# Attention and gated FFN on one core: another order for the LayerNorm prologue and for the first group's KV units

## The chip, the cores and the metric

One core of a Trainium2 chip. The metric is the device time of one execution in microseconds, lower is better; the median of three runs of the kernel before is 1325.37 us (1324.14 to 1325.52).

## The reference, cut to what matters

```python
xn = _layernorm(x)                        # x: 1024 tokens x 512
q = xn @ Wq.T                             # 32 heads of 128
k = xn @ Wk.T; v = xn @ Wv.T              # 8 groups of 128, four heads share one
q = rmsnorm(q, q_norm_w); k = rmsnorm(k, k_norm_w)
scores = q k^T / sqrt(128) + slope * (k_pos - q_pos), causal
s = softmax(scores) v @ Wo.T
g = silu((silu(xn @ gate) * (xn @ up)) @ down)     # gate, up, down dequantised from integers
return x + s * g
```

## The kernel before, in words

Every fp32 operand of a product is split in two parts, hi (rounded to the matmul's fp32r) and lo (the rest). ScalarE writes the hi part, VectorE or GpSimd (POOL) the lo part, and TensorE (PE) runs three products, hi*hi, hi*lo and lo*hi.

**Prologue.** SyncE loads the eight tiles of x (128 tokens each, L285), while ScalarE's own queue loads the KV weights of group 0 (L536). For each tile VectorE computes the statistics (`ln_stats`, L635, and `ln_variance`, L640 to L643), two tiles at a time; POOL takes the power -0.5 (L414) and normalises both rows in place (`ln_rows`, L417). PE transposes the normalised tile (`ln_transposes`, L1012), ScalarE writes `xh` (L547) and VectorE `xl` (`ln_lo`, L650). PE has 14 + 1 + 3 matmuls on zeros (`idle_matmuls`, L1005) before and between the first two transposes and the first product. A "KV unit" (`kv_proj`, L967) is 24 matmuls of 256 columns that give K and V of two token tiles; a "Q unit" (`q_proj`, L950) is 12 matmuls of 512 columns that give Q^T of one head for 512 tokens, called qc1 for the later half of the tokens and qc0 for the earlier. The order of PE's units in the prologue stands in `PRO`: kv0, kv1, kv2, the Q unit qc1_0, kv3, with the transposes of later x tiles placed inside the units. K of group 0 is copied from PSUM by VectorE (L751), squared and summed by ScalarE (`k_squares`, L518), and scaled by POOL (`k_norm`, L403 and L406); then PE transposes it (`first_k_transposes`) and ScalarE and VectorE split it (L530, L735).

**Heads.** A group has four heads. Within a head eight query tiles (idx 0 is the last tile, 1024 keys long) pass through scores (PE, L926 to L929), logits (VectorE adds the bias tile that POOL made, L687), exp (ScalarE, L497), normalise (VectorE, L693 and L696), transposes of the probabilities (PE, `lot`, L907), their split (ScalarE L487, VectorE L671) and the product with V (PE, `values`, L945). Between these PE's queue holds projections: the Q units of this and the next head, the output projection of the two heads before (`w_unit`; in heads 0 and 1 there is none yet), and one KV unit of the next group per head (kv0 to kv3 of group 1 in heads 0 to 3). The order is written out by hand on each engine; `group_order` gives the sequence in which the two PSUM banks `O` are handed on, and `Places` turns it into semaphore counts. A unit waits until the one before it in this list has left its bank's partner (`take`, L892). The first group is written apart from the six steady ones (a loop over heads, unrolled) and the last, which has no KV units. The feed-forward part follows and is not touched.

Of the kernel before, what the change touches and what calls it, by code (L numbers as in the profile page):

```python
# [111 lines left out]
PRO = ["kv0", "kv1", "kv2", "qc1_0", "kv3"]  # L112


def group_order(first, last):


    out = []
    for j in range(PER):
        nx = (j + 1) % PER  # L120
        more = not (last and j == PER - 1)
        prev, w = not (first and j == 0), not (first and j < 2)
        out += [f"qc0_{j}"] + [f"v0_{j}"] * prev + [f"w0_{j}", f"w1_{j}"] * w
        if first and j == 0:
            out += ["kv0", "qc1_1"]
# [56 lines left out]
def f(ap):  # L182

    return ap.bitcast(F32)
# [10 lines left out]
def attention(nc, stack, keep, x, wq, wkv, wo, slopes, qkw, mats, down_sc):  # L195
# [32 lines left out]
    rstd = sb("rstd", [P, QT])  # L228
    kss, kms, kinv = sb("kss", [P, QT]), sb("kms", [P, QT]), sb("kinv", [P, QT])
# [8 lines left out]

    LN_BANKS = [T[0][:, :], T[1][:, :]] + [S[n // 2][:, n % 2 * CH:(n % 2 + 1) * CH] for n in range(4)]
# [5 lines left out]
    setup, ln_st, ln_mv, ln_var, ln_rstd, xn_ready = (  # L245
        sem("setup"), sem("ln_st"), sem("ln_mv"), sem("ln_var"), sem("ln_rstd"), sem("xn_ready"))
# [81 lines left out]
    def _(pool):  # L328
# [70 lines left out]
        def k_norm(g, c):  # L399
            n = NC * g + c  # L400
            cs = slice(c * CT, (c + 1) * CT)
            pool.wait_ge(kms_ready, n + 1)
            g_.tensor_tensor(kinv[:, cs], kms[:, cs], cst[:, 0:1].to_broadcast([P, CT]),  # L403
                             ALU.pow).then_inc(kinv_ready, 1)
            pool.wait_ge(kinv_ready, n + 1)
# [4 lines left out]
        def ln_rows(n):  # L410
# [69 lines left out]
    def _(act):  # L480
# [55 lines left out]
        act.dma_start(wkv_in[:, :, :], wkv[0]).then_inc(wkv_ld, 16)  # L536
        act.wait_ge(wkv_ld, 16)
        for n in range(2):
            ks = slice(2 * n, 2 * n + 2)
            a_.activation(wkv_h[:, ks, :], wkv_in[:, ks, :], ACT.Copy).then_inc(wkv_hi, 1)  # L540
        wq_hi_part(0)
# [8 lines left out]
        ln_hi(range(0, 5))  # L550
        k_squares(pro, ["kv0"], 0)
        ln_hi(range(5, 7))
        k_squares(pro, ["kv1"], 0)
        ln_hi(range(7, 8))
        k_squares(pro, ["kv2"], 0)
        q_hi(pro, "qc1_0")
# [3 lines left out]
        k_squares(pro, ["kv3"], 0)  # L560
        wkv_hi_part(1)

        def group(g, kind):
# [4 lines left out]
            for j in range(PER):  # L568
# [10 lines left out]
                q_hi(at, f"qc0_{j}")  # L579
                if kind == "first" and j == 0:  # L580
                    act.wait_ge(kt_ready, 2)
                    kT_hi_part(0, slice(CH, TOK))
                if j == 0:
                    exp(h, 0)
# [22 lines left out]
                if kind != "last":  # L607
# [3 lines left out]
                lots(h, 2)  # L611
                v_hi(at, f"v1_{j}", j)
# [16 lines left out]
    def _(dve):  # L629
# [35 lines left out]
        ln_lo(range(3, 4))
# [105 lines left out]
        def group(g, kind):
# [6 lines left out]
            for j in range(PER):  # L778
# [17 lines left out]
                elif kind == "first":  # L796
                    q_lo(at, f"qc0_{j}")
                    dve.wait_ge(kt_hi, 2)
                    kT_lo_part(slice(CH, TOK))
                    logits(h, 0)  # L800
# [41 lines left out]
                if not last and (prev or j > 0):  # L842
# [6 lines left out]
                lots(h, 3)  # L849
                normalise(h, 6)  # L850
# [26 lines left out]
    def _(pe):  # L877
# [53 lines left out]

        def values(at, name, h, wait, between=None):
# [67 lines left out]
        pro = Places("pro")  # L1000

# [5 lines left out]
        def ln_transposes(i):  # L1007
            pe.wait_ge(xn_ready, i + 1)
# [6 lines left out]

        pe.wait_ge(warm, 1)
# [522 lines left out]
```

## Time and profile before

| | us |
|---|---|
| median of 3 runs | 1325.37 |
| profiled execution, its own time | 1325.52 |
| its span, first to last instruction | 1323.4 |
| PE busy | 1287.3 (97%) |
| VectorE (DVE) busy | 970.1 (73%) |
| ScalarE (ACT) busy | 649.8 (49%) |
| GpSimd (POOL) busy | 710.2 (54%) |

All times in the trace are from the span's start. PE rows are matmuls, PEld rows weight loads. The last entry in brackets is how long the engine sat idle before the instruction, and who released it. Matmul durations overlap (they are pipelined), so lengths of stretches of PE are read from start to start.

### The profile page before, as it was taken

The numbers are of one execution on the slowest core, as the hardware profiler recorded it, in microseconds if no ns is written. First come the engines' busy times: TensorE is split into PE (matmuls) and PEld (weight loads), VectorE is DVE, ScalarE is ACT, GpSimd is POOL, SyncE is SP. The second block draws the span as 40 slices with busy tenths as digits, with TensorE's granted clock in tenths as the row PEclk, the third lists the DMA queues.
The fourth block names the chain that finished last, engine by engine and source line by source line (L and its number), as shares of the span: only waits on it lengthen the run. The fifth ranks groups of instructions, "written<-read, shape, count | busy, mean of one in ns | idle before, by whom it ended". The sixth has DMA issues, their size and how long they took to land. (4 is left out here: it accounts for less than half of the span.)

```text
span 1323.4 us, 20983 instructions
## 1 busy us (share of the span) xinstructions
PE 1287.3 (97%) x7138; PEld 1105.0 (83%) x7138; DVE 970.1 (73%) x2072; ACT 649.8 (49%) x1422; POOL 710.2 (54%) x755
## 2 busy tenths in 40 slices
PE   7899999999999999999999999999999989999997
PEld 6778888888888888888888888888888878888886
DVE  4678787778777877787778777877788855555556
ACT  3555565556555555555555555555565523222222
POOL 8645464546455545554555455545555625555553
PEclk8899999999999999999999999999999999999999
DMA  3000000000000000100000000000020036455441
GB/s 121 17 17 17 33 17 17 17 32 17 17 17 32 17 17 17 33 17 17 17 33 17 17 16 33 17 17 17 17 64 20 5 77 194 128 127 127 127 127 64
DMA packets 29468, 57.88 MB, mean 44 GB/s; under 512 B 3648, under 2 KB 3648, under 8 KB 29248
## 3 DMA queue, kind: packets, MB, share of 16 engines
q1 hardware_dynamic: 29232, 56.16, 14.9%
q8 instruction: 54, 0.88, 0.3%
q10 hardware_dynamic: 144, 0.52, 0.1%
q14 instruction: 38, 0.31, 0.1%
HBM read 54.57 MB, written 2.10 MB: 43 GB/s over the span
## 5 line engine op out<-in xcount | busy, mean ns | idle before, releaser
L396 POOL TENSOR_TENSOR pb<-rel,coef 128x1024 f32<-128x1024 f32 (+7 forms) x256 | 293.7, 1162 | 123.9 <-PE T L907 118.1
L497 ACT ACTIVATE pb<-pb,low 128x1024 f32<-128x1024 f32 (+7 forms) x256 | 198.9, 777 | 188.6 <-DVE low L687 186.9
L487 ACT ACTIVATE pt_h<-T 128x512 fp32r<-128x512 f32 (+3 forms) x384 | 185.9, 486 | 115.0 <-PE T L907 111.6
L671 DVE TENSOR_TENSOR pt_l<-T,pt_h 128x512 fp32r<-128x512 f32 (+3 forms) x384 | 210.4, 551 | 41.2 <-ACT pt_h L487 41.1
L687 DVE CUSTOM_DVE_ANT_0 pb<-S,pb,ninv 128x1024 f32<-128x1024 f32 (+7 forms) x256 | 207.8, 812 | 40.7 <-PE S L929 35.8
L907 PE MATMUL T<-ident,pb 128*128 128x128 f32 x1152 | 190.7, 275 | 14.9 <-DVE pb L696 8.4
L907 PEld LDWEIGHTS T<-ident,pb 128*128 128x128 f32 x1152 | 141.6, 141 | 53.6 <-issue 14.0
L696 DVE TENSOR_SCALAR pb<-pb,rinv 128x1024 f32<-128x1024 f32 (+7 forms) x256 | 172.5, 674 | 9.0
L926 PE MATMUL S<-kT_h,q_h 128*128 128x512 f32 (+2 forms) x384 | 142.0, 370 | 0.0
L945 PE MATMUL O<-pt_h,v_h 128*128 128x512 f32 (+2 forms) x384 | 140.7, 366 | 1.0 <-DVE pt_l L671 1.0
L373 POOL TENSOR_TENSOR inv<-ms,cst 128x4 f32<-128x4 f32 x64 | 76.2, 1191 | 120.8 <-DVE ms L719 120.8
L352 POOL TENSOR_TENSOR wo_l<-wo_in,wo_h 128x512 fp32r<-128x512 f32 x32 | 41.5, 1297 | 184.3 <-ACT wo_h L534 184.3
L945 PE MATMUL O<-pt_h,v_l 128*128 128x512 f32 (+2 forms) x384 | 133.4, 347 | 0.0
L945 PE MATMUL O<-pt_l,v_h 128*128 128x512 f32 (+2 forms) x384 | 132.9, 346 | 0.0
L927 PE MATMUL S<-kT_l,q_h 128*128 128x512 f32 (+2 forms) x384 | 129.2, 344 | 0.0
L929 PE MATMUL S<-kT_h,q_l 128*128 128x512 f32 (+2 forms) x384 | 111.4, 344 | 0.0
L886 PE MATMUL O<-xh,wq_h 128*128 128x512 f32 x256 | 109.2, 427 | 0.7 <-DVE xl L650 0.7
L886 PE MATMUL O<-oT_h,wo_h 128*128 128x512 f32 x256 | 107.1, 418 | 0.0
L886 PE MATMUL O<-xh,wq_l 128*128 128x512 f32 x256 | 101.0, 394 | 0.0
L886 PE MATMUL O<-oT_h,wo_l 128*128 128x512 f32 x256 | 100.7, 393 | 0.0
L886 PE MATMUL O<-oT_l,wo_h 128*128 128x512 f32 x256 | 100.6, 393 | 0.0
L886 PE MATMUL O<-xl,wq_h 128*128 128x512 f32 x256 | 100.5, 393 | 0.0
(148 smaller groups left out, 2898.7 us busy)
## 6 DMA issues: line engine op xcount, KB each, us to landing
wq_in<-in_wq SPq DMA_DIRECT2D x32, 256.0 KB, 2.8
wo_in<-in_wo SPq DMA_DIRECT2D x32, 256.0 KB, 2.6
stage<-in_wkv SPq DMA_DIRECT2D x7, 512.0 KB, 3.9
stage<-in_gate_w SPq DMA_DIRECT2D x14, 256.0 KB, 2.6
stage<-in_gate_z SPq DMA_DIRECT2D x14, 256.0 KB, 3.6
stage<-in_gate_s SPq DMA_DIRECT2D x14, 256.0 KB, 5.2
stage<-in_up_w SPq DMA_DIRECT2D x14, 256.0 KB, 5.3
stage<-in_up_z SPq DMA_DIRECT2D x14, 256.0 KB, 6.4
```

The costliest lines, as they stand in the source:

```text
L396: g_.tensor_tensor(pbuf(idx, t), rel[:, TOK - w:TOK], coef[:, t:t + 1].to_broadcast([P, w]), ALU.mult).then_inc(bias_ready, 1)
L487: a_.activation(pt_lot(pt_h, t, n), bank[:, 0:m * P].rearrange("p (k w) -> p k w", w=P), ACT.Copy).then_inc(tr_hi, 1)
L497: a_.activation(pbuf(idx, t), pbuf(idx, t), ACT.Exp, bias=low[:, idx:idx + 1], scale=-1.0, accum_out=rsum[:, idx:idx + 1]).then_inc(exps_r ...
L671: v_.tensor_tensor(pt_lot(pt_l, t, n), bank[:, 0:m * P].rearrange("p (k w) -> p k w", w=P), f(pt_lot(pt_h, t, n)), ALU.subtract).then_inc( ...
L687: v_.tensor_tensor_reduce(out=pbuf(idx, t), in0=S[idx % 2][:, BASE[t]:BASE[t] + (t + 1) * P], in1=pbuf(idx, t), scale=ninv[:, t:t + 1], sc ...
L696: v_.tensor_scalar(pbuf(idx, t), pbuf(idx, t), rinv[:, idx:idx + 1], None, ALU.mult).then_inc(probs_ready, 1)
L886: ins = mm(out, a, b, start=(n == 0), stop=(n == 3 * len(terms) - 1))
L907: ins = nc.tensor.transpose(bank[:, k * P:(k + 1) * P], pbuf(idx, t)[:, (k0 + k) * P:(k0 + k + 1) * P], ident[:, :])
L926: mm(out, q[:, qs], kT_h[:, k0:k0 + w], start=True, stop=False)
L927: mm(out, q[:, qs], kT_l[:, k0:k0 + w], start=False, stop=False)
L929: ins = mm(out, q[:, qs], kT_h[:, k0:k0 + w], start=False, stop=True)
L945: ins = mm(o, v[:, kt, :], pt[:, a:a + w], start=(kt + i == 0), stop=(kt == n - 1 and i == 2))
```

## The change

The loads: `wkv[0]` is issued by SyncE between x tiles 3 and 4 and no longer by ScalarE at the start. LayerNorm rows 0, 1, 2, 4 and 6 are normalised by VectorE with the same two-scalar instruction that POOL had; rows 3, 5 and 7 by ScalarE as scale * x + shift, where POOL computes the shift, 128x1, from mean and rstd. POOL keeps the power and loses the eight 128x512 rows; of the KV weights' lo part it makes one half, VectorE the other. In kv0 the products with the lo weights come last, and the first ones wait for halves of the hi weights. The zero matmuls are 11 + 4 in place of 14 + 1 + 3. In the prologue kv3 comes before the Q unit qc1_0. K of group 0 is scaled by VectorE, tile by tile (eight instructions of 128x128), and POOL only takes the power. The first bias tile (128x1024) of head 0 is made by VectorE. The first scores of head 0 stand after 12 of the 24 matmuls of group 1's kv0, where they stood after 20, and their last products alone wait for the lo part of Q. Head 0 runs KV units kv0 and kv1 of group 1, head 1 runs kv2 and kv3, heads 2 and 3 none.

```diff
-PRO = ["kv0", "kv1", "kv2", "qc1_0", "kv3"]
+PRO = ["kv0", "kv1", "kv2", "kv3", "qc1_0"]
+FIRST_KV = (["kv0", "kv1"], ["kv2", "kv3"], [], [])
...
     def _(sp):
         for i in range(QT):
+            if i == 4:
+                sp.dma_start(wkv_in[:, :, :], wkv[0]).then_inc(wkv_ld, 16)
             sp.dma_start(xs[:, i, :], x[i]).then_inc(x_in[i], 16)
...
# POOL
-            for i in (2 * n, 2 * n + 1):
-                g_.tensor_scalar(xs[:, i, :], xs[:, i, :], mv[:, i, 0:1], rstd[:, i:i + 1], ALU.subtract,
-                                 ALU.mult).then_inc(xn_ready, 1)
+            if n > 0:
+                i = 2 * n + 1
+                g_.tensor_scalar(shift[:, i:i + 1], mv[:, i, 0:1], rstd[:, i:i + 1], -1.0, ALU.mult,
+                                 ALU.mult).then_inc(ln_shift, 1)
         pool.wait_ge(setup, SETUP + 5)
-        wkv_lo_half(0)
         ln_rows(0)
-        wkv_lo_half(1)
         ln_rows(1)
+        wkv_lo_first()
         ln_rows(2)
+        wq_lo(0)
         ln_rows(3)
-        wq_lo(0)
-        k_norm(0, 0)
+        k_inv(0, 0)
+        k_inv(0, 1)
         pool.wait_ge(tab_in, 32)
         norms(0, 1)
-        k_norm(0, 1)
-        bias(0, 0)
+        pool.wait_ge(bias_ready, 1)
         bias(0, 1)
...
# ScalarE
-        act.dma_start(wkv_in[:, :, :], wkv[0]).then_inc(wkv_ld, 16)
...
+        def ln_rows(i):
+            act.wait_ge(ln_shift, XN_ACT.index(i) + 1)
+            a_.activation(xs[:, i, :], xs[:, i, :], ACT.Identity, bias=shift[:, i:i + 1],
+                          scale=rstd[:, i:i + 1]).then_inc(xn_by_act, 1)
+        ln_hi(range(0, 1))
...
+        ln_hi(range(1, 2))
+        ln_rows(3)
+        ln_hi(range(2, 4))
+        wq_hi_part(0)
+        ln_rows(5)
+        ln_hi(range(4, 6))
         k_squares(pro, ["kv0"], 0)
...
+        ln_rows(7)
+        ln_hi(range(6, 8))
+        k_squares(pro, ["kv1", "kv2", "kv3"], 0)
...
# VectorE
+        def ln_rows(i):
+            dve.wait_ge(ln_rstd, i // 2 + 1)
+            v_.tensor_scalar(xs[:, i, :], xs[:, i, :], mv[:, i, 0:1], rstd[:, i:i + 1], ALU.subtract,
+                             ALU.mult).then_inc(xn_by_dve, 1)
...
+        ln_stats(range(2, 3))
+        ln_rows(0)
+        ln_rows(1)
+        ln_stats(range(3, 4))
         ln_variance(1)
...
+        ln_lo(range(1, 2))
+        ln_rows(2)
+        ln_stats(range(4, 5))
+        ln_lo(range(2, 4))
+        ln_stats(range(5, 6))
         ln_variance(2)
+        first_kv_copy(0)
+        ln_rows(4)
+        ln_stats(range(6, 8))
         ln_variance(3)
+        ln_lo(range(4, 6))
+        ln_rows(6)
+        first_kv_copy(1)
+        ln_lo(range(6, 8))
...
+        def first_k_norm(c):
+            dve.wait_ge(kinv_ready, c + 1)
+            for k in range(c * CT, (c + 1) * CT):
+                ins = v_.tensor_scalar(kv[:, k, 0:HD], kv[:, k, 0:HD], kinv[:, k:k + 1], None, ALU.mult)
+            ins.then_inc(kn_ready, 1)
...
+                    dve.wait_ge(coef_ready, 2)
+                    v_.tensor_scalar(pbuf(0, TILES[0]), rel[:, :], coef[:, QT - 1:QT], None, ALU.mult
+                                     ).then_inc(bias_ready, 1)
...
# PE
         pe.wait_ge(warm, 1)
-        idle_matmuls(14)
+        idle_matmuls(11)
         pe.wait_ge(setup, SETUP + 5)
         ln_transposes(0)
-        idle_matmuls(1)
         ln_transposes(1)
-        idle_matmuls(3)
-        for n in range(3):
-            kv_proj(pro, f"kv{n}", 0, {6: [lambda n=n: ln_transposes(2 * n + 2)], 18: [lambda n=n: ln_transposes(2 * n + 3)]})
+        idle_matmuls(4)
+        first_kv0()
+        for n in (1, 2):
+            kv_proj(pro, f"kv{n}", 0, {8: [lambda n=n: ln_transposes(2 * n + 2)], 16: [lambda n=n: ln_transposes(2 * n + 3)]})
+        kv_proj(pro, "kv3", 0)
         pe.wait_ge(tr_lo, QT)
-        q_proj(pro, "qc1_0", 0)
-        kv_proj(pro, "kv3", 0, {4: [lambda: first_k_transposes(0)],
-                                14: [lambda: squares(pro.hi("qc1_0"), 1, QT, T[1])]})
+        q_proj(pro, "qc1_0", 0, {4: [lambda: first_k_transposes(0)]})
...
-                q_proj(at, "qc0_0", 0)
-                kv_proj(at, "kv0", 1, {6: [lambda: first_k_transposes(1)], 20: [first_scores]})
+                q_proj(at, "qc0_0", 0, {8: [lambda: squares(pro.hi("qc1_0"), 1, QT, T[1])]})
+                kv_proj(at, "kv0", 1, {2: [lambda: first_k_transposes(1)], 12: [first_scores]})
...
-                if not last and (prev or j > 0):
-                    kv_proj(at, f"kv{j}", g + 1, {3 * KT: [squares1]})
+                now = FIRST_KV[j][j == 0:2 - j] if kind == "first" else [f"kv{j}"] * (not last)
+                if now:
+                    kv_proj(at, now[0], g + 1, {3 * KT: [squares1]})
                 elif more:
                     squares1()
                 scores(h, 6)
                 lots(h, 3)
+                if kind == "first" and j == 1:
+                    kv_proj(at, "kv3", 1)
                 values(at, f"v1_{j}", h, g + 1 if j == 0 else None, {12: [lambda h=h: lots(h, 2)]})
```

## Rows read from the trace of the kernel before

**Rows 1.** The page: the span, and part 1, busy time of each engine.
```profile
span 1323.4 us, 20983 instructions
PE 1287.3 (97%) x7138; PEld 1105.0 (83%) x7138; DVE 970.1 (73%) x2072; ACT 649.8 (49%) x1422; POOL 710.2 (54%) x755
```

**Rows 2.** Waits of PE, 0 to 200 us: us in total, times, longest.
```profile
PE T L1012 <- POOL s_acc L417: 4.5, 3, 3.3
PE T L907 <- DVE pb L696: 3.2, 4, 1.8
PE T L907 <- DVE pt_l L671: 3.1, 4, 1.1
PE T L964 <- DVE pt_l L671: 1.8, 1, 1.8
PE O L886 <- DVE w_l L769: 1.2, 1, 1.2
PE S L1012 <- POOL s_acc L417: 1.1, 2, 0.7
PE O L886 <- DVE xl L650: 0.7, 1, 0.7
```

**Rows 3.** Timeline of PE: start us, us, line, operation, count, [idle before <-releaser].
```profile
1.58 6.25 PE L1005 MATMUL O<-pt_h 128*128 128x512 f32 x14 [1.58 <-DVE pt_h L653]
11.12 1.08 PE L1012 MATMUL T<-ident,s_acc 128*128 128x128 f32 x4 [3.30 <-POOL s_acc L417]
...
22.12 0.66 PE L1012 MATMUL S<-ident,s_acc 128*128 128x128 f32 x4 [0.70 <-POOL s_acc L417]
...
50.53 1.32 PE L907 MATMUL T<-ident,pb 128*128 128x128 f32 x8 [1.82 <-DVE pb L696]
...
65.44 0.63 PE L964 MATMUL T<-ident,sq 128*128 128x128 f32 x4 [1.81 <-DVE pt_l L671]
```

**Rows 4.** DMA issues, 0 to 60 us: KB each, median us from issue to landing.
```profile
s_acc<-in_x SPq DMA_DIRECT2D x8, 256.0 KB, 5.7
...
stage<-in_wkv ACTq DMA_DIRECT2D x1, 512.0 KB, 5.2
```

**Rows 5.** Windows: busy us of PE, PEld, DVE, ACT, POOL; granted clock; DMA share; GB/s.
```profile
7.00:8.00 1.00, 0.83 (x3) 0.20 (x1) 0.97 (x5) 0.06 (x1) 0.97 (x1) 1.00 1.05 404
...
11.00:12.00 1.00, 0.88 (x5) 0.91 (x5) 0.00 (x0) 0.63 (x1) 1.00 (x1) 0.50 0.19 58
...
17.50:18.00 0.50, 0.50 (x5) 0.50 (x4) 0.00 (x0) 0.00 (x0) 0.50 (x1) 0.67 0.00 0
...
52.00:53.00 1.00, 1.00 (x5) 0.91 (x4) 0.66 (x2) 1.00 (x3) 0.00 (x0) 0.50 0.02 8
...
58.50:59.00 0.50, 0.50 (x4) 0.46 (x3) 0.50 (x2) 0.13 (x1) 0.50 (x1) 0.71 0.00 0
```

**Rows 6.** Timeline of all engines: statistics, power and rows of the first two tiles.
```profile
5.74 1.45 DVE L635 BATCH_NORM_STATS2 stats<-s_acc 128x6 f32<-128x512 f32 x2 [4.21 <-DMA s_acc<-in_x]
...
8.08 0.72 POOL L414 TENSOR_TENSOR rstd<-var_e,cst 128x2 f32<-128x2 f32 x1
8.90 4.14 POOL L417 TENSOR_SCALAR s_acc<-s_acc,mv,rstd 128x512 f32<-128x512 f32 x2
```

**Rows 7.** Timeline of PE: first matmuls of qc1_0, of kv3 and of qc0_0.
```profile
31.18 0.50 PE L886 MATMUL O<-xh,wq_h 128*128 128x512 f32 x1 [0.70 <-DVE xl L650]
...
34.03 0.28 PE L886 MATMUL O<-w_h,xh 128*128 128x256 f32 x1
...
37.76 0.40 PE L886 MATMUL O<-xh,wq_h 128*128 128x512 f32 x1
```

**Rows 8.** Timeline of DVE: one-input instructions, POOL idle and POOL busy.
```profile
65.39 0.49 DVE L696 TENSOR_SCALAR pb<-pb,rinv 128x512 f32<-128x512 f32 x1
...
71.24 1.37 DVE L696 TENSOR_SCALAR pb<-pb,rinv 128x256 f32<-128x256 f32 x1
```

**Rows 9.** Waits of PE, 940 to 1010 us, in the last group: us, times, longest.
```profile
PE T L907 <- DVE pt_l L671: 0.8, 2, 0.4
```

More of the change, by code:

```diff
@@ L123, in group_order @@
         out += [f"qc0_{j}"] + [f"v0_{j}"] * prev + [f"w0_{j}", f"w1_{j}"] * w
-        if first and j == 0:
-            out += ["kv0", "qc1_1"]
+        if first:
+            out += ["kv0"] * (j == 0) + [f"qc1_{nx}"] + [f"w2_{j}"] * w + FIRST_KV[j][j == 0:]
         else:
@@ L228, in attention @@
     rstd = sb("rstd", [P, QT])
+    shift = sb("shift", [P, QT])
     kss, kms, kinv = sb("kss", [P, QT]), sb("kms", [P, QT]), sb("kinv", [P, QT])
@@ L548, in ln_hi @@
                               ACT.Copy).then_inc(tr_hi, 1)
-        ln_hi(range(0, 5))
-        k_squares(pro, ["kv0"], 0)
[L552 to L556, printed above, removed]
+        def ln_rows(i):
[3 more added lines that the diff above has]
+        ln_hi(range(0, 1))
+        act.wait_ge(wkv_ld, 16)
+        for n in range(2):
+            ks = slice(2 * n, 2 * n + 2)
+            a_.activation(wkv_h[:, ks, :], wkv_in[:, ks, :], ACT.Copy).then_inc(wkv_hi, 1)
+        ln_hi(range(1, 2))
[4 more added lines that the diff above has]
+        ln_hi(range(4, 6))
+        k_squares(pro, ["kv0"], 0)
+        ln_rows(7)
+        ln_hi(range(6, 8))
+        k_squares(pro, ["kv1", "kv2", "kv3"], 0)
         act.wait_ge(qk_ready, 1)
@@ L559, in _ @@
         kT_hi_part(0, slice(0, CH))
-        k_squares(pro, ["kv3"], 0)
         wkv_hi_part(1)
+        q_hi(pro, "qc1_0")
         def group(g, kind):
@@ L582, in group @@
                     kT_hi_part(0, slice(CH, TOK))
+                q_hi(at, f"qc0_{j}")
                 if j == 0:
@@ L606, in group @@
                 exp(h, 5)
-                if kind != "last":
+                if kind == "first":
+                    k_squares(at, FIRST_KV[j][:2 - j], 1)
+                elif kind != "last":
                     k_squares(at, [f"kv{j}"], g + 1)
@@ L611, in group @@
                 lots(h, 2)
+                if kind == "first" and j == 1:
+                    k_squares(at, ["kv3"], 1)
                 v_hi(at, f"v1_{j}", j)
@@ L769, in _ @@
         v_.tensor_tensor(wkv_l[:, :, :], wkv_in[:, :, :], f(wkv_h[:, :, :]), ALU.subtract).then_inc(wkv_split, 1)
+        first_k_norm(1)
+        q_lo(pro, "qc1_0")
+        mean_sq(0, 1, QT, T[1])
         def group(g, kind):
@@ L841, in group @@
                 normalise(h, 5)
-                if not last and (prev or j > 0):
+                if kind == "first":
+                    kv_copy(at, FIRST_KV[j][j == 0:2 - j], 1)
+                elif not last:
                     kv_copy(at, [f"kv{j}"], g + 1)
@@ L849, in group @@
                 lots(h, 3)
+                if kind == "first" and j == 1:
+                    kv_copy(at, ["kv3"], 1)
                 normalise(h, 6)
@@ L930, in scores, with first_scores @@
             ins.then_inc(scores_ready, 1)
+        pro = Places("pro")
+        def first_scores():
+            qs = slice(TOK - P, TOK)
+            for k0 in range(0, TOK, CH):
+                pe.wait_ge(kt_lo, k0 // CH + 1)
+                ks = slice(k0, k0 + CH)
+                mm(S[0][:, ks], q_h[:, qs], kT_h[:, ks], start=True, stop=False)
+                mm(S[0][:, ks], q_h[:, qs], kT_l[:, ks], start=False, stop=False)
+            pe.wait_ge(out_free, pro.n("qc1_0"))
+            for k0 in range(0, TOK, CH):
+                ks = slice(k0, k0 + CH)
+                ins = mm(S[0][:, ks], q_l[:, qs], kT_h[:, ks], start=False, stop=True)
+            ins.then_inc(scores_ready, 1)
         def values(at, name, h, wait, between=None):
@@ L1106, in group @@
                 lots(h, 3)
+                if kind == "first" and j == 1:
+                    kv_proj(at, "kv3", 1)
                 values(at, f"v1_{j}", h, g + 1 if j == 0 else None, {12: [lambda h=h: lots(h, 2)]})
```

89 lines of the change are left out of this document (46 added, 43 removed).

## The prediction

> **What bounds the kernel now.** I read the page first: PE is busy 97% of a span of 1323.4 us, and VectorE, the next unit of work beside it, at 73% [rows 1]. So a change gains only what it takes from PE's idle time or from time in which PE works slowly. Next the waits of PE, narrowed to the first 200 us [rows 2]: 15.6 us of idle time stand there, 5.6 of it at the transposes of x, which wait for the rows that POOL normalises, 1.2 for the lo part of group 1's KV weights, 0.7 for xl, and 8.1 in the first heads, where PE waits for VectorE. Beyond 200 us there is nothing of this size. Then the timeline of PE [rows 3]: it runs zero matmuls up to 7.8 us, sits idle until 11.12, and reaches the transposes of head 0's probabilities at 50.53 after another 1.82. From there on the order of work is nearly the same in both kernels, so I forecast this landmark, and the KV units apart from it. Last the windows [rows 5]: the granted clock falls to half (1.2 GHz) at 11 us, after 3.3 us of idle PE, and is back at 17.7; it falls again at 52 us, soon after the wait of 1.82, and is back at 58.7. The 14 zero matmuls take 0.446 us each (6.25 / 14 [rows 3]), 512 columns at about 1.2 GHz, while the window before the fall shows 1.00: they too run at the lower level.
>
> **The change, step by step.** All in the time of the profiled execution, 1325.52, 0.1 above the median.
>
> *Loads.* Before, x tile 0 and the 512 KB of KV weights land at about the same time, 5.74 for the tile, by VectorE's first start [rows 6], and 0.73 + 5.2 for the weights. At the 404 GB/s of the windows [rows 5] 512 KB are 1.3 us. With the weights behind tile 3 the first tile should land at 4.4 and the second 0.65 (256 KB) later, at 5.05; the weights, 1.5 MB into the queue, at about 7.7. Bounds: nothing gained, if starting up sets the 5.0 to 6.0 us that a tile takes [rows 4], and 1.6. I take 1.3, since the tiles behind the first follow at this rate. The Trainium skill ("DMA: Bandwidth & Descriptors", section "Issuing engines are not separate DMA queues") says that transfers of all issuing engines run on the same 16 DMA engines and interleave; by that the weights did hold up x and the 1.3 us stand, and the trace agrees so far, as both landed together.
>
> *First row.* Before, the second statistics start at 6.46 (5.74 + 0.72, half of the pair's 1.45), the power at 8.08, 1.6 later, the row at 8.90, 0.8 later [rows 6], and the transpose at 11.12. After: 5.05, power 6.7, result 7.5, then a row on VectorE. The nearest row is a one-tensor instruction of the same size and type, 0.49 [rows 8], against 2.07 on POOL [rows 6]. PE starts the first transpose at about 8.1 (3.0 earlier), after 1.6 idle in place of 3.3, since 11 zero matmuls end at 6.5. On ScalarE a row should take what its other 128x512 passes do, about 0.6.
>
> *First transpose to the transpose of tile 4.* Before this takes 11.0 us (11.12 to 22.12). After, PE starts with two transposes (0.8 each at the low clock) and four zero matmuls (1.7), so kv0 starts at 11.4. Its first 12 matmuls are 2.6 at half clock, the other 12 between 1.4 and 2.6, with the transposes of tiles 2 and 3 between: tile 3 starts at 16.0 if the clock comes back on the way, at 15.2 if it does earlier, at 17.4 if not. Behind tile 3 there is a chain, which is the new bound: transpose 0.4, hi part 0.6 and lo part 0.7 (estimates: passes over 128x512, between the 0.49 of rows 8 and the 0.72 of rows 6), statistics of tile 5 0.7, variance 0.6 (with the statistics it is 1.6 less hand-overs), power 0.8, row 0.5, then tile 4. It is 4.3 us, and PE has only 8 matmuls (1 us) to put beside it, so it waits some 2.5 us there. That gives tile 4 at 20.3, against 22.12: 1.8 earlier, bounds 2.8 and 0.4. The 3.0 us at the first row are largely given back because VectorE has statistics, lo parts and rows in one line.
>
> *The shared port.* The row that is nearest for contention is a one-input instruction of VectorE of 256 columns that took 1.37 while POOL was in a bias tile [rows 8]; half the size of the 0.49 one. POOL now has wkv_lo, wq_lo and the shifts beside VectorE's rows. I charge 0.1, bounds 0 and 1.2, because the rows start right when POOL hands over its power, and wq_lo comes behind the shift. The Trainium skill ("SBUF — State Buffer", section "SBUF: two separate sides") says that the pair of ports that VectorE and GpSimd share is an exclusive lock for a whole instruction, and counts VectorE's two-input instructions too. By that the lo parts on VectorE would queue behind POOL as well, and tile 4 would come up to 1.3 later; I have not seen a two-input one stretched that way in the rows, so the sum goes by 0.1.
>
> *Tile 4 to head 0's first transposes.* Before 28.4 us (22.12 to 50.53). The work of PE is the same set: kv1 to kv3, the Q units (2.85 each, 34.03 - 31.18 [rows 7]), kv0 of group 1, the first scores; kv3 with eight small transposes is 3.73 [rows 7]. After, two matmuls of kv1 lie already before tile 4 (0.2). The waits in it are 0.8 (tile 6, one of the three of T L1012), 0.7 (xl), 1.2 (weights) and 1.8 [rows 2, 3]. The first three go, 2.7, and with them about 0.5 of refilling the pipe: rows come at 0.5 to 0.6 now, and the weights' lo part is made during qc1_0 and qc0_0. The moved K scaling costs VectorE eight small instructions beside qc1_0; kept at nothing, at worst 0.5. The wait of 1.82 stays: behind the first scores come logits, exp, second logits and normalise, and these have the same lengths. The earlier scores (8 matmuls, 0.9) are balanced by the first bias tile, which VectorE now makes just ahead of them (1.0 or less, twice the 0.49), and by POOL's second one, which waits for it. A small new wait of 0.2 stands at the second half of kT_l. Sum: 28.4 - 0.2 - 2.7 - 0.5 + 0.2 = 25.2, so the landmark is at 20.3 + 0.1 + 25.2 = 45.6 in place of 50.5: 4.9 us.
>
> *KV units.* A KV unit is 2.8 us: kv3's 3.73 [rows 7] less its eight transposes, 0.9 as an estimate (eight span 1.32 with the pipe's end in it [rows 3]). In head 0 the added one stands where PE waits 1.81 [rows 3] for VectorE; it cannot start before VectorE has copied kv0, 0.5 into the wait, so 1.3 is covered and 1.5 is added. In head 1 the added unit stands where PE is full: 2.8 added, 0.3 of it won back at a later wait. Heads 2 and 3 lose 2.8 each. Do they really get shorter? The last group has no KV units at all and shows only 0.8 of waits of this kind for its heads [rows 9], so I charge 0.4 for two heads. 1.5 + 2.5 - 5.6 + 0.4 = -1.2. The copies (0.6) and squares (0.9) move with the units; VectorE has gaps there, and 0.2 of it is charged: -1.0.
>
> Sum: -4.9 - 1.0 = -5.9, and 1325.5 - 5.9 = 1319.6.
>
> **The rivals.**
> *A third half-clock stretch.* PE is now idle twice close together, 0.7 before kv1 and some 2.5 before tile 4. The fall at 52 us came after 1.82 [rows 5]; against it speaks that the waits of 0.7 to 0.8 between 20 and 31 us [rows 2, 3] left the clock full. A stretch like those seen lasts 6.7 us and costs up to half, 3.3: 1322.9.
> *The second half-clock stretch vanishes.* Other work lies around head 0's first wait, and if the clock stays full, the 6.7 us from 52 to 58.7 lose their cold part. VectorE is not far behind there (a wait of up to 1.1 in between [rows 2]), so 2: 1317.6.
> *Loads do not come earlier*, and the reordering of the queue does not do what it says: the start costs 1.3 more, all of it through the chain: 1320.9.
> *Slower.* The clock stays at half beyond tile 4, since there are fewer zero matmuls (15 for 18) and a wait in front of each step. The prologue's work for PE is then twice as long. It decides from the point where half the time at the low level exceeds the 5.9 us gained, that is 11.8 us more of it, past 32 us. With all of the 25 us to the landmark at half the kernel would take up to 1331. Against it: from 20 to 50 us PE is busy nearly throughout, and in the kernel before such work had full clock from 17.7 on.
>
> **The numbers.** Forecast 50%, third stretch 18%, second vanishes 14%, loads 14%, slower 4%. The likeliest is 1319.6. The range takes in the early arrival with warm clock below (2.8 in place of 1.8 at tile 4, and the lost stretch, together 3.6) and the third stretch with its full price above: 1316.0 to 1323.0. A measurement of this kernel can tell about 0.2% from no change, 2.65 us, so faster means under 1322.7: 0.84, since half of the third stretch's cases lie just above that line; within 0.2% 0.12; slower 0.04.
>
> **What would show it.** First statistics at 4.4, first transpose at 8.1 and without POOL rows; transposes of tile 4 at 20.3 with a wait of about 2.5 released by a VectorE row; no wait for w_l; head 0's first transposes at 45.6 with a wait near 1.8; squares of head 0 no longer waiting; heads 2 and 3 shorter by 2.8 each with under 0.4 of new waits. I am wrong if VectorE's first start is still at 5.7, if one-input rows on VectorE take over 1 us, if the windows from 18 to 40 us show half clock, or if heads 0 and 1 grow by more than 4.

## The result and the profile after

The changed kernel takes 1317.86 us (median of 5 runs, 1317.14 to 1318.63) beside 1325.2 us for the kernel before: a ratio of 0.9949, 95% interval 0.9938 to 0.996, so 7.3 us faster by the medians where 5.7 (from 1325.37 to 1319.6) was forecast. The interval is 5.3 to 8.2 us, so the times alone do not tell the two apart. In a second set of executions (e8) the medians were 1317.45 and 1324.0, 6.6 us apart, with the same ratio, 0.9949 (0.9932 to 0.9965). The kernel before took 1323.6 to 1324.5 us in 34 of its 49 later executions and 1324.8 to 1325.6 in 11, as in the profiled one (1325.52): about 1 us of the 7.3 hangs on that. The profiled execution of after has a span of 1316.1 us, 7.3 shorter than [rows 1].

The waits of PE over 0 to 200 us, after (us in total, times, longest):

```profile
PE T L957 <- DVE pt_l L718: 3.9, 6, 1.1
PE T L957 <- DVE pb L743: 3.5, 4, 2.2
PE S L1079 <- DVE s_acc L678: 2.0, 1, 2.0
...
PE O L1098 <- POOL w_l L360: 1.1, 1, 1.1
PE T L1079 <- DVE s_acc L678: 0.7, 1, 0.7
PE O L936 <- DVE xl L672: 0.6, 1, 0.6
PE O L936 <- DVE stage L773: 0.5, 1, 0.5
```

Against [rows 2], the 5.6 us behind POOL's rows are gone, and 2.7 behind VectorE's rows stand there; the wait for group 1's `w_l` of 1.2 is gone, and another of 1.1, for group 0's lo weights, has come (L1098, in kv0, at 11.68). The wait of 1.8 at head 0's squares is gone as well; 0.5 is left before the KV unit that now stands in it. The half-clock stretch of the kernel before from 11 to 17.7 us is gone too. It is not known to have cost anything there: PE's waits of 0.4 to 0.8 us for POOL's rows stand inside it and behind it. The timeline of PE, the rows that answer to [rows 3]:

```profile
1.57 5.06 PE L1069 MATMUL O<-pt_h 128*128 128x512 f32 x11 [1.57 <-DVE pt_h L675]
7.32 1.07 PE L1079 MATMUL T<-ident,s_acc 128*128 128x128 f32 x8 [0.68 <-DVE s_acc L678]
8.14 1.15 PE L1069 MATMUL O<-pt_h 128*128 128x512 f32 x4
...
18.52 0.66 PE L1079 MATMUL S<-ident,s_acc 128*128 128x128 f32 x4 [2.02 <-DVE s_acc L678]
...
43.47 1.32 PE L957 MATMUL T<-ident,pb 128*128 128x128 f32 x8 [2.24 <-DVE pb L743]
...
70.22 0.33 PE L957 MATMUL T<-ident,pb 128*128 128x128 f32 x1 [0.37 <-DVE pb L743]
...
102.85 0.33 PE L957 MATMUL T<-ident,pb 128*128 128x128 f32 x1 [0.38 <-DVE pb L743]
...
169.49 1.32 PE L957 MATMUL T<-ident,pb 128*128 128x128 f32 x8 [0.47 <-DVE pb L743]
```

The same places in both traces, the last three being the one place in heads 1 and 2, and the end of head 3:

| | before | after | lead |
|---|---|---|---|
| first transpose | 11.12 | 7.32 | 3.8 |
| transposes of x tile 4 | 22.12 | 18.52 | 3.6 |
| landmark (head 0's first transposes) | 50.53 | 43.47 | 7.06 |
| in head 1 | 75.71 | 70.22 | 5.5 |
| in head 2 | 105.46 | 102.85 | 2.6 |
| end of head 3 | 176.55 | 169.49 | 7.06 |

So in these two traces the prologue gave all of it. Heads 0 and 1 take 1.6 and 2.9 longer, heads 2 and 3 together 4.45 less, and the move of the KV units ends at nothing. VectorE and POOL in the prologue, after:

```profile
3.46 1.31 DVE L657 BATCH_NORM_STATS2 stats<-s_acc 128x6 f32<-128x512 f32 x2 [1.94 <-DMA s_acc<-in_x]
...
6.64 0.99 DVE L678 TENSOR_SCALAR s_acc<-s_acc,mv,rstd 128x512 f32<-128x512 f32 x2
...
9.65 0.69 DVE L696 TENSOR_TENSOR w_l<-stage,w_h 128x512 fp32r<-128x512 f32 x1 [0.35 <-ACT w_h L564]
...
10.87 1.04 DVE L678 TENSOR_SCALAR s_acc<-s_acc,mv,rstd 128x512 f32<-128x512 f32 x1
...
14.47 0.69 DVE L672 TENSOR_TENSOR xl<-S,xh 128x512 fp32r<-128x512 f32 x1 [1.97 <-ACT xh L551]
...
15.99 0.68 DVE L657 BATCH_NORM_STATS2 stats<-s_acc 128x6 f32<-128x512 f32 x1
...
17.92 0.54 DVE L678 TENSOR_SCALAR s_acc<-s_acc,mv,rstd 128x512 f32<-128x512 f32 x1 [0.23 <-POOL rstd L424]
```

```profile
9.60 0.80 POOL L428 TENSOR_SCALAR shift<-mv,rstd 128x1 f32<-128x1 f32 x1
...
20.97 0.26 POOL L428 TENSOR_SCALAR shift<-mv,rstd 128x1 f32<-128x1 f32 x1
```

The first row pair takes 0.99 on VectorE where POOL took 4.14 [rows 6]. The chain that I had forecast as the new bound ahead of tile 4 can be read off: VectorE stands idle for 1.97 ahead of 14.47, waiting for tile 2's hi part, and the statistics of tile 5, for which x is long there, come only after two lo parts (15.99). Row 4 follows at 17.92, and PE starts on it at 18.52 after 2.02 idle.

### The profile page after: what moved, and what is told of

It reads as the page before. It is cut to its first block and busy times, and to the rows that moved or that the text cites. A ratio compares the mean times of both kernels' runs of the same rounds, so it can differ in the third digit from the quotient of the medians.

```text
span 1316.1 us, 20988 instructions
## 1 busy us (share of the span) xinstructions
PE 1283.2 (98%) x7135; PEld 1102.1 (84%) x7135; DVE 974.1 (74%) x2087; ACT 651.2 (49%) x1425; POOL 689.7 (52%) x746
## 5 line engine op out<-in xcount | busy, mean ns | idle before, releaser
L403 POOL TENSOR_TENSOR pb<-rel,coef 128x896 f32<-128x896 f32 (+1 forms) x255 | 292.0, 1159 | 128.0 <-PE T L957 120.6
L976 PE MATMUL S<-kT_h,q_h 128*128 128x512 f32 x382 | 141.3, 370 | 0.0
L977 PE MATMUL S<-kT_l,q_h 128*128 128x512 f32 x382 | 128.6, 344 | 0.0
L979 PE MATMUL S<-kT_h,q_l 128*128 128x512 f32 x382 | 110.8, 344 | 0.0
```

Source lines behind the costliest of these rows:

```text
L403: g_.tensor_tensor(pbuf(idx, t), rel[:, TOK - w:TOK], coef[:, t:t + 1].to_broadcast([P, w]), ALU.mult).then_inc(bias_ready, 1)
L976: mm(out, q[:, qs], kT_h[:, k0:k0 + w], start=True, stop=False)
L977: mm(out, q[:, qs], kT_l[:, k0:k0 + w], start=False, stop=False)
```

## The experiments

The landmark below is always the start of head 0's first transposes of probabilities, and "the changed kernel" is 43.47 for it and a median of 1317.86 us (1317.45 in e8).

### e1: the weights' load on ScalarE's queue again

```diff
-            if i == 4:
-                sp.dma_start(wkv_in[:, :, :], wkv[0]).then_inc(wkv_ld, 16)
...
+        act.dma_start(wkv_in[:, :, :], wkv[0]).then_inc(wkv_ld, 16)
```

> The changed kernel with the load of group 0's KV weights issued by ScalarE at the start again. Theory A (the weights' 512 KB held up x): first statistics at 5.7 instead of 3.5, first transpose at 9.6 instead of 7.3, and the landmark (head 0's first transposes of probabilities) at 45.7 instead of 43.5, 2.2 us slower in all; if the idle time ahead of the first transpose (6.6 to 9.6 us) also lets the clock fall, 1 to 3 us more. Rival B (the start of the loads sets the time, the order of the queues nothing): first statistics stay at 3.5 and the time stays. Rival C (weights earlier help kv0 as much as x later hurts): the wait of 1.1 for the lo part of the weights goes and the loss is about 1.

1321.47 us, ratio to before 0.9977 (0.9968 to 0.9987). Timeline of PE, and a window (PE, PEld, DVE, ACT, POOL busy, granted clock, DMA share, GB/s):

```profile
9.10 1.94 PE L1078 MATMUL T<-ident,s_acc 128*128 128x128 f32 x8 [2.46 <-DVE s_acc L677]
...
21.10 0.97 PE L1078 MATMUL S<-ident,s_acc 128*128 128x128 f32 x4 [2.01 <-DVE s_acc L677]
...
47.54 1.43 PE L956 MATMUL T<-ident,pb 128*128 128x128 f32 x8 [2.25 <-DVE pb L742]
```

```profile
21.00:24.00 3.00, 2.90 (x15) 2.90 (x16) 2.32 (x7) 1.41 (x2) 2.31 (x4) 0.55 0.21 54
```

Statistics start at 5.63 again, so the 512 KB did hold up x: theory A, and B falls. Rival C had its wait right: none for the lo weights is left on PE. But the loss is not 1: it is 4 us (1321.47 beside 1317.45, with 1324.07 and 1324.0 for the kernel before), with 1.8 at the first transpose, 2.6 at tile 4, 4.1 at the landmark. The last 1.5 of it goes with a stretch at half clock from 21 us, right after the wait of 2.01 at tile 4, which the changed kernel's first trace did not have there (but see e8).

### e2: one KV unit per head

```diff
-FIRST_KV = (["kv0", "kv1"], ["kv2", "kv3"], [], [])
+FIRST_KV = (["kv0"], ["kv1"], ["kv2"], ["kv3"])
```

(and the places on PE, VectorE and ScalarE that follow from it.)

> The changed kernel with one KV unit of group 1 in each of heads 0 to 3, as before the change. Theory A (the traces of before and after: the lead is 7.06 at the landmark and 7.06 again at the end of head 3): time within 0.5 us of the changed kernel; heads 0 and 1 shorter by 1.6 and 2.9, heads 2 and 3 longer by 2.2 each. Rival B (my sum: the move is worth 1.0, because the unit in head 0 fills a wait): 1.0 us slower than the changed kernel, heads 2 and 3 longer by 2.8 each less 0.2.

1318.32 us, ratio 0.9959 (0.9945 to 0.9973), which does not tell it from the changed kernel's 0.9949. Its timeline of PE:

```profile
43.78 1.75 PE L953 MATMUL T<-ident,pb 128*128 128x128 f32 x8 [2.25 <-DVE pb L741]
...
70.36 0.33 PE L953 MATMUL T<-ident,pb 128*128 128x128 f32 x1 [0.45 <-DVE pb L741]
...
100.09 0.33 PE L953 MATMUL T<-ident,pb 128*128 128x128 f32 x1 [0.35 <-DVE pb L741]
...
171.21 1.32 PE L953 MATMUL T<-ident,pb 128*128 128x128 f32 x8 [0.47 <-DVE pb L741]
```

Heads 2 and 3 take 71.1 (100.09 to 171.21) beside 66.6 after, head 1 29.7 beside 32.6: the unit moves as planned. Head 0 takes 26.6, although it has the shorter list: its windows show two stretches at half clock in this execution (0.75 in 43 to 46, 0.68 in 46 to 49, then 0.54 in 52 to 55). So this trace alone cannot price the move; e5 to e8 do.

### e3: all rows on POOL, the rest as changed

```diff
-            if n > 0:
-                i = 2 * n + 1
-                g_.tensor_scalar(shift[:, i:i + 1], mv[:, i, 0:1], rstd[:, i:i + 1], -1.0, ALU.mult,
-                                 ALU.mult).then_inc(ln_shift, 1)
+            for i in (2 * n, 2 * n + 1):
+                g_.tensor_scalar(xs[:, i, :], xs[:, i, :], mv[:, i, 0:1], rstd[:, i:i + 1], ALU.subtract,
+                                 ALU.mult).then_inc(xn_by_dve, 1)
```

(The rows on VectorE and ScalarE are taken out with it.)

> The changed kernel with all eight LayerNorm rows on POOL, as before the change; all else as changed. Theory A (the rows on POOL are most of the 7 us): eight rows at 2.08, four powers, wkv_lo and wq_lo make one line of 22 us on POOL from 5.4 on, so the last tile is transposed at about 26 instead of 24, and the landmark is at 46 to 47 instead of 43.5: 3 us slower. Rival B (VectorE's line of statistics and lo parts is the bound either way): within 1 us of the changed kernel. Rival C (the order of the loads gave all of it): no loss at all.

1329.22 us, ratio 1.0039 (1.0025 to 1.0053): 11.4 to 11.8 slower than the changed kernel and slower than before. Every theory missed this. POOL's timeline:

```profile
11.47 4.67 POOL L427 TENSOR_SCALAR s_acc<-s_acc,mv,rstd 128x512 f32<-128x512 f32 x2
...
22.92 0.72 POOL L424 TENSOR_TENSOR rstd<-var_e,cst 128x2 f32<-128x2 f32 x1 [5.55 <-DVE var_e L661]
```

POOL is not busy without a break, as I had counted; it waits 5.55 us for the variance of tiles 4 and 5. In the new order that variance stands behind lo parts of tiles 2 and 3, those wait for PE's kv0, kv0 waits for the lo weights (PE is idle for 2.16 there), and these stand behind four rows on POOL. So in the new order each engine waits for the next around PE: with VectorE's rows of 0.5 us it gained, with POOL's of 2.07 it lost. The landmark is at 53.76, 10.3 later. How much of that its two stretches at half clock ahead of the landmark add (8.8 to 15.6 and 25.9 to 29.3 us) is not separated.

### e4: 3 zero matmuls instead of 11

```diff
-        idle_matmuls(11)
+        idle_matmuls(3)
```

> The changed kernel with 3 zero matmuls at the start instead of 11, so that PE is idle from about 3 to 7.3 us. Theory A (my sum missed because the clock was full from the first transpose on, where I had it at half until 14 to 17 us): with the long idle time the windows from 7 us on show 0.50 or matmuls at twice the spacing, transposes of tile 4 come at 19.5 to 21 instead of 18.5, and the kernel is 1 to 3 us slower. Rival B (VectorE's chain hides PE's clock): the low clock shows, but tile 4 stays at 18.5 and the time within 0.5 us.

1319.6 us, ratio 0.9961 (0.9947 to 0.9975), not told from the changed kernel. Its timeline of PE:

```profile
7.15 1.94 PE L1079 MATMUL T<-ident,s_acc 128*128 128x128 f32 x8 [3.93 <-DVE s_acc L678]
8.75 1.84 PE L1069 MATMUL O<-pt_h 128*128 128x512 f32 x4
...
11.55 0.74 PE L1098 MATMUL O<-w_l,xh 128*128 128x256 f32 x4
...
14.12 0.60 PE L1079 MATMUL S<-ident,s_acc 128*128 128x128 f32 x4
...
18.52 0.66 PE L1079 MATMUL S<-ident,s_acc 128*128 128x128 f32 x4 [2.03 <-DVE s_acc L678]
```

Eight transposes and four zero matmuls take 1.94 and 1.84 where they took 1.07 and 1.15: PE runs at the lower level here, though the clock column reads 1.00. Still tile 3 starts at 14.12, tile 4 at 18.52 and the landmark at 43.48, to a hundredth as in the changed kernel. By 11.55 the spacing is the fast one (four in 0.74), and the slow matmuls before fill just the wait of 1.1 for the lo weights. So in this execution (1317.88 us) rival B: the clock ahead of 11 us costs nothing. The times are weaker: the median is 1.7 to 2.2 above the changed kernel's, and three of the five executions took 1319.6 to 1320.4, so a loss in other executions, as theory A had it, is not excluded.

### e5: the rows alone, in the kernel before

The normalisation of rows on VectorE (0, 1, 2, 4, 6) and ScalarE (3, 5, 7), with the loads, POOL's and PE's orders and the heads left as before. VectorE's part of the edit:

```diff
+        ln_rows(0)
+        ln_rows(1)
...
         ln_lo(range(0, 2))
+        ln_rows(2)
...
         ln_lo(range(2, 3))
+        ln_rows(4)
...
         ln_lo(range(3, 4))
+        ln_rows(6)
```

> The kernel before with one part of the change alone: rows 0, 1, 2, 4, 6 normalised on VectorE and 3, 5, 7 on ScalarE, POOL making the shifts. Theory A (the rows on POOL held the whole prologue: their eight times 2.08 us are its bound, whatever the order of the rest): transpose of tile 4 at 17 to 18 instead of 22.1, landmark at 45 to 46 instead of 50.5, 4 to 5 us faster than before. Rival B (the rows pay only together with the new order of loads and of POOL's and VectorE's lines): under 2 us faster.

1320.06 us, ratio 0.997 (0.996 to 0.9981): 4.0 faster than before. Its timeline of PE:

```profile
10.52 1.04 PE L1040 MATMUL T<-ident,s_acc 128*128 128x128 f32 x4 [2.89 <-DVE s_acc L670]
...
18.54 0.60 PE L1040 MATMUL S<-ident,s_acc 128*128 128x128 f32 x4
...
45.55 1.32 PE L932 MATMUL T<-ident,pb 128*128 128x128 f32 x8 [1.82 <-DVE pb L721]
...
69.35 0.33 PE L932 MATMUL T<-ident,pb 128*128 128x128 f32 x1 [0.59 <-DVE pb L721]
...
170.25 1.32 PE L932 MATMUL T<-ident,pb 128*128 128x128 f32 x8 [0.47 <-DVE pb L721]
```

Theory A: the landmark comes 5.0 earlier. Tile 4 is at 18.54, as early as in the full change, although the first transpose starts 3.2 later; there is no wait ahead of it, because here the statistics of tiles 4 and 5 stand ahead of the lo parts. The weights' wait of 1.21 and the one of 0.7 for xl remain; that is most of the 2.1 to the full change's landmark.

### e6: the order of the loads alone, in the kernel before

```diff
         for i in range(QT):
+            if i == 4:
+                sp.dma_start(wkv_in[:, :, :], wkv[0]).then_inc(wkv_ld, 16)
...
-        act.dma_start(wkv_in[:, :, :], wkv[0]).then_inc(wkv_ld, 16)
```

> The kernel before with the order of the loads alone changed (KV weights behind x tile 3). Theory A (POOL's line decides: wkv_lo stands ahead of its first row there, so the later weights hold up every row): first statistics at 3.5, first transpose at about 12.6 instead of 11.1, 1.5 us slower than before. Rival B (x early is a gain by itself, as in e1, which lost 4 us without it): 1 to 3 us faster.

1326.33 us, ratio 1.0015 (1.0005 to 1.0025): 2 us slower than before, where theory A had 1.5. Statistics start at 3.33, but the first transpose only at 13.09:

```profile
10.87 4.14 POOL L419 TENSOR_SCALAR s_acc<-s_acc,mv,rstd 128x512 f32<-128x512 f32 x2
```

```profile
13.09 1.09 PE L1013 MATMUL T<-ident,s_acc 128*128 128x128 f32 x4 [6.72 <-POOL s_acc L419]
```

The lo part of the weights stands ahead of POOL's first power, so later weights hold up every row. The same edit is worth 4 us inside the change (e1) and costs 2 alone.

### e7: K's scaling and the first bias tile on POOL, the rest as changed

```diff
-        k_inv(0, 0)
-        k_inv(0, 1)
+        k_norm(0, 0)
+        k_norm(0, 1)
...
-        pool.wait_ge(bias_ready, 1)
+        bias(0, 0)
...
-        first_k_norm(0)
...
-        first_k_norm(1)
```

(VectorE's bias instruction is gone too.)

> The changed kernel with the scaling of K of group 0 and the first bias tile of head 0 back on POOL. Theory A (as the prediction charged them: both lie beside PE's work): within 0.5 us of the changed kernel, landmark at 43.0 to 44.0. Rival B (POOL's longer K scaling, 1.0 to 1.7 against 0.9, and a bias tile of 1.9 against 0.7 stand in the chain to head 0's first logits): landmark 1 to 2 us later.

1318.73 us, ratio 0.9958 (0.9944 to 0.9972), and the landmark at 44.29. That is later than theory A's 43.0 to 44.0, but beside e8, whose clock ran the same way, it is 0.3 earlier, so by the traces theory A: both lie beside PE's work. The median is 0.9 to 1.3 above the changed kernel's, and the intervals overlap. These two parts of the change brought nothing that these runs can see.

### e8: the changed kernel again

> The changed kernel itself, beside the others on one chip, to see how far its landmarks and its time move between executions. Every theory: first statistics 3.3 to 4.0, transposes of tile 4 at 18.3 to 19.0, landmark at 43.3 to 44.0, ratio to before 0.994 to 0.996.

1317.45 us, ratio 0.9949. Span 1315.6, half a microsecond from the first, but the landmark is outside what was expected. Timeline of PE, and windows:

```profile
18.30 0.66 PE L1079 MATMUL S<-ident,s_acc 128*128 128x128 f32 x4 [2.03 <-DVE s_acc L678]
...
44.59 1.32 PE L957 MATMUL T<-ident,pb 128*128 128x128 f32 x8 [2.24 <-DVE pb L743]
...
69.83 0.33 PE L957 MATMUL T<-ident,pb 128*128 128x128 f32 x1 [0.37 <-DVE pb L743]
...
169.12 1.31 PE L957 MATMUL T<-ident,pb 128*128 128x128 f32 x8 [0.47 <-DVE pb L743]
```

```profile
19.00:21.00 2.00, 2.00 (x13) 2.00 (x11) 1.42 (x5) 0.62 (x2) 1.51 (x3) 0.54 0.27 47
21.00:23.00 2.00, 2.00 (x13) 2.00 (x12) 1.08 (x3) 1.68 (x6) 0.02 (x1) 0.61 0.25 92
```

In this execution the clock falls after the wait of 2.03 at tile 4, for some 3.4 us, and is full in head 0; in the first it was full from tile 4 to the landmark and at 0.50 from 45 to 51 us, 6.8 us in all. From tile 4 to the landmark it takes 26.29 instead of 24.95, head 0 takes 25.24 instead of 26.75, and the sum is nearly the same. So a half-clock stretch cost 1.3 us in the one place and 1.5 in the other, and the landmark of one execution carries that much chance.

One row of VectorE differs from the first execution. It is the lo part of the weights, with both its inputs in SBUF, here beside POOL's own `w_l`, which runs for 1.29 us from 9.42:

```profile
9.90 1.37 DVE L696 TENSOR_TENSOR w_l<-stage,w_h 128x512 fp32r<-128x512 f32 x1 [1.00 <-ACT w_h L564]
```

In the first execution the same instruction took 0.69, and POOL's `w_l` started only behind it (10.36).

The traces also price the KV units, if executions with the same clock in head 0 are compared (us between the places of the table above):

| | units per head | half clock in head 0 | head 0 | head 1 | heads 2 and 3 | landmark to end of head 3 |
|---|---|---|---|---|---|---|
| before | 1, 1, 1, 1 | 6.8 | 25.18 | 29.75 | 71.09 | 126.02 |
| changed, first | 2, 2, 0, 0 | 6.8 | 26.75 | 32.63 | 66.64 | 126.02 |
| e5 | 1, 1, 1, 1 | none | 23.80 | 29.76 | 71.14 | 124.70 |
| e6 | 1, 1, 1, 1 | none | 23.68 | 29.75 | 71.13 | 124.56 |
| e7 | 2, 2, 0, 0 | none | 25.23 | 32.61 | 66.64 | 124.48 |
| e8 | 2, 2, 0, 0 | none | 25.24 | 32.63 | 66.66 | 124.53 |

The move is worth 0 to 0.2 us.

### e9, e10, e11, e12: filling the waits that are left

e9 takes VectorE's chain ahead of tile 4 apart: statistics and variance of tile 5 come before the lo part of tile 2.

```diff
         ln_rows(2)
-        ln_stats(range(4, 5))
-        ln_lo(range(2, 4))
-        ln_stats(range(5, 6))
+        ln_stats(range(4, 6))
         ln_variance(2)
-        first_kv_copy(0)
+        ln_lo(range(2, 3))
         ln_rows(4)
+        ln_lo(range(3, 4))
+        first_kv_copy(0)
```

> The changed kernel with statistics and variance of tile 5 on VectorE ahead of the lo part of tile 2, and row 4 right behind that lo part. Theory A (the wait of 2.0 ahead of the transposes of tile 4 is VectorE's line, statistics behind lo parts that themselves wait for PE): that wait goes, tile 4 at 16.4 to 16.8 instead of 18.5, landmark at 41.5 instead of 43.5 and 1.5 to 2 us faster than the changed kernel. Rival B (the time comes back as waits for POOL or ScalarE at tiles 5 to 7): under 0.7 us faster.

1315.43 us, ratio 0.9938 (0.9921 to 0.9955). Timeline of PE in e9:

```profile
15.99 0.60 PE L1079 MATMUL S<-ident,s_acc 128*128 128x128 f32 x4
```

Theory A: no wait at tile 4, which starts 2.5 earlier, and all of it reaches the landmark (40.89) and the end of head 3 (166.93 for 169.49). By the medians it is 2.0 to 2.4 faster than the changed kernel; the intervals of the ratios overlap, so it is the traces that show it.

e10 has in addition ScalarE split half the KV weights ahead of tile 0's hi part, and POOL make their lo part ahead of the second power.

```diff
         ln_rows(0)
+        wkv_lo_first()
         ln_rows(1)
-        wkv_lo_first()
...
-        ln_hi(range(0, 1))
...
+            if n == 0:
+                ln_hi(range(0, 1))
```

> As e9, and in addition ScalarE splits the first half of the KV weights ahead of the hi part of tile 0, and POOL makes their lo part ahead of the second power. Theory A: the wait of 1.1 for the lo weights in kv0 goes and the landmark is at 40.5 to 41 instead of 41.5. Rival B (the weights land at 7.7 or later and the hi part of tile 0 waits for them): kv0 starts later by as much, no gain, or up to 0.5 loss.

1314.19 us, ratio 0.993 (0.9914 to 0.9947), landmark at 40.26, 0.6 earlier than e9. The wait of 1.1 for `w_l` is gone, but one of 0.7 for tile 0's xl has come in its place, so half each of the two theories; the ratios do not tell it from e9. The medians are 1.2 apart, but this trace shows no stretch at half clock, where that of e9 has one of 6.8 us in head 0.

e11 is e9 with V of group 0 split at the end of the prologue (ScalarE and VectorE), so that VectorE can copy kv0 and kv1 ahead of the third logits of head 0, and with kv1 of group 1 ahead of the landmark, kv2 in the next wait, kv3 in head 1.

```diff
-FIRST_KV = (["kv0", "kv1"], ["kv2", "kv3"], [], [])
+FIRST_KV = (["kv2"], ["kv3"], [], [])
...
                     squares0()
+                    kv_proj(at, "kv1", 1)
                 lots(h, 7)
...
                 lot(h, 7, 0)
+                if kind == "first" and j == 0:
+                    kv_copy(at, ["kv0", "kv1"], 1)
                 logits(h, 2)
```

> As e9, and in addition V of group 0 is split at the end of the prologue, so that KV unit kv1 of group 1 can stand in the wait ahead of the landmark and kv2 in the next one; kv3 in head 1, none in heads 2 and 3. Theory A (a unit is worth what it covers: 2.2 at the first place, 1.8 at the second): the landmark itself comes 0.6 later than in e9, the end of head 3 about 2.8 earlier than in e9, and the whole is 4 to 5 us faster than the changed kernel. Rival B (VectorE's two copies and the V split, 1.2 each, delay head 0's logits as much as PE gains): within 1 us of e9.

1312.97 us, ratio 0.9916 (0.99 to 0.9933): 4.5 faster than the changed kernel, as theory A had it. The wait at the landmark is gone; the end of head 3 is at 163.81 beside 166.93 in e9, but part of these 3.1 us is the clock (3.4 us at half in head 0 beside 6.8). A wait of 2.10 has come at 46.04, at the later transposes of head 0, where 1.10 was (VectorE's two copies stand ahead of it).

e12 has all three edits.

> The changed kernel with all three edits: tile 5's statistics first (e9), the KV weights' split ahead of tile 0's hi part (e10), and the units kv1 and kv2 of group 1 in head 0's waits (e11). Theory A (the edits fill different waits and add up; e10 was 1.2 faster than e9, e11 2.5 faster than e9): 1311 to 1312.5, ratio to before 0.990 to 0.991, first weights' wait gone and the landmark about 1 us earlier than in e11. Rival B (the earlier lead of e10 runs into VectorE's V split and coefficients, which do not come earlier): no faster than e11.

1311.57 us, ratio 0.9904 (0.9887 to 0.992), within what A said: the fastest version, 13.4 us under the kernel before beside it. (The ratio of 0.9904 gives 12.7.) Its interval meets that of e11, its first transposes of tile 4 are no earlier (15.97 beside 15.82), and neither is the landmark (41.34 beside 41.21), where A had 1 us, so what e10's edit adds here is open. What e11's edit is worth can be read against e10, since neither trace has a stretch at half clock; the end of head 3 in e10 and then in e12:

```profile
164.75 1.32 PE L958 MATMUL T<-ident,pb 128*128 128x128 f32 x8 [0.47 <-DVE pb L744]
```

```profile
162.50 1.32 PE L957 MATMUL T<-ident,pb 128*128 128x128 f32 x8 [0.83 <-DVE pb L743]
```

It is 2.25 us. What is left of PE's waits over 0 to 200 us in e12, beside the one before the zero matmuls and two of 0.8 in all at x:

```profile
PE T L957 <- DVE pt_l L718: 5.5, 7, 2.1
...
PE T L957 <- DVE pb L743: 1.2, 2, 0.8
PE O L1092 <- DVE xl L672: 1.2, 1, 1.2
```

## Why the prediction was right, and where it was not

**The bound and the place.** PE's waits in the first 50 us were where the gain lay, and the rows on POOL were its largest part: e5 alone gives 4.0 of the 6.6 us that the change gave beside it (e8).

**Loads.** The forecast was 4.4 for the first statistics; they start at 3.46. The bound above, 1.6 earlier, was too near: it is 2.3. I took only the 1.3 us of the 512 KB at full rate off, and the first statistics start 0.9 ahead of what that gives; why is open. e1 shows the weights' load as the cause, and e6 that the gain is there only if nothing at the head of POOL's line waits for the weights. I did not see in the prediction that this term hung on another.

**First row and tile 4.** First transpose at 7.3 for 8.1, mostly the loads. From there to tile 3 I had 7.9 us, and it took 6.8; from tile 3 to tile 4 I had 4.3, and it took 4.4, with 2.0 of idle PE for the 2.5 forecast. The 1.1 was a clock assumed at half up to 14 us and added in full. In the trace PE ran fast from 7 us on (four zero matmuls in 1.15). But e4, where it was at half until about 11, has tile 3 at 14.12 as well: the lo weights were the later input of kv0, and their wait of 1.1, missing from the sum, took up the slow matmuls. So the step had the clock's return too late and the weights' wait left out, and the second would have hidden the first.

**The port.** Row 2 took 1.04 on VectorE for the 0.54 of row 4 [rows 8 had 0.49], beside POOL's 1.27 of `w_l`. The port was charged 0.1, and the row cost 0.5, but where it was not waited for: in e8 it took 0.53 and tile 4 came at 18.30. POOL's shift of one column took 0.80 beside VectorE's two-input `w_l` and 0.26 alone. The sentence of the Trainium skill ("SBUF — State Buffer", section "SBUF: two separate sides"), that an instruction with two SBUF inputs takes the shared pair as well, agrees with that, and with the 1.37 us of VectorE's `w_l` in e8; I had weighed it as unseen. I had also read it too widely: the sentence counts two inputs in SBUF. One input of the lo parts of x is in PSUM, and they kept 0.68 beside POOL's `w_l` (10.26 in the first execution).

**Tile 4 to the landmark.** 24.95 for 25.2. The waits named as going went, and the one that stays was 2.24 for 1.8 (1.82 in e5 and e6, with the old order; what adds the 0.4 was not taken apart).

**KV units.** This is the term that failed: -1.0 forecast, 0 to -0.2 measured (e5 and e6 beside e7 and e8). Head 0 was right (1.4 to 1.6, for 1.5). Head 1 gave back nothing of the 0.3. Heads 2 and 3 lost 4.5 and not 5.6 - 0.4: two new waits of 0.43 stand in them, of the kind of [rows 9]; where the other 0.3 went is open. PE has a gap of over 1 us for a unit only in head 0, and the unit was put where 0.5 of the gap is lost to the copy of kv0. e11 and e12 show what the move can be worth with units in the waits proper: 2.5 us more than e9 by the medians, 2.25 by the traces of e10 and e12.

**Rivals.** The third half-clock stretch (18%) and the vanishing second one (14%) are both true, in one execution (e8): a stretch stands at tile 4 and none in head 0. I had priced them at 3.3 and 2, apart; one cost 1.3 and the other 1.5. The second needs no change at all: e5 and e6, whose heads are those of the kernel before, have no stretch in head 0 either. The rival of slower did not come; the loads came earlier.

The sum was -5.9, against -7.3 (-6.6 in e8): 2.1 us too little in the prologue, 0.8 to 1.0 too much in the heads. That the total came within 0.7 to 1.4 us is partly luck, since the two misses have opposite signs. Two numbers of the prediction do not follow from its own terms. Below 1319.6 it adds 1.0 (tile 4) and 2 (the stretch) to 3.6; they make 3.0, so the lower end would be 1316.6. And its chances give 0.87 for faster (0.50 + 0.14 + 0.14 + half of 0.18), not 0.84. The measured 1317.86 lies inside either way.

## What to carry to other kernels

A load order, a queue order and a faster instruction are one edit: the same load order cost 2 us alone and gave 4 with the rest, and the same new order with POOL's rows was 11 slower than with VectorE's. Before work is moved into a thin stretch, find the wait it is to fill, and what holds the buffer that it needs. In a line that mixes work whose input is long there (statistics) with work that waits for another engine (lo parts), the first goes ahead: that reordering was worth 2 us here (e9). And a price read from one pair of traces is checked for where the half-clock stretches lie in each, since one is worth as much as many an edit.

## What the runs showed of the hardware that was not expected

The granted clock read 1.00 over windows in which PE ran slow: in e4 four matmuls of 512 columns take 1.84 us at 8.75, and 1.15 in the changed kernel; its eleven at the start take 5.06, 0.46 each, where those of its Q unit start 0.23 apart (30.68 and 30.91). So in these traces the clock ahead of the first record of a fall is to be read from the spacing.

The place and the length of a half-clock stretch differ between executions of one kernel (3.4 us from 19.4 in e8, 6.8 from 44.8 in the first), with the span within 0.5 us; twice the length did not cost twice as much (1.3 and 1.5). And an instruction of VectorE with two inputs in SBUF took 1.37 us beside POOL's `w_l` and 0.69 without it, while one with an input in PSUM kept 0.68.
